# A transformer layer on one core: attention's loop over batches written out, and the next batch's front moved to the first third of a batch

## The reference

```
a  = layernorm(x);  h = rmsnorm(a, norm_w)
q, k, v = h@Wq, h@Wk, h@Wv                         # 16 heads of 8
lin = linear_attention_causal(taylor(q@Wqf), taylor(k@Wkf), v)
win = softmax attention over the last 64 keys
x  = x + a + concat(lin, win) @ Wout               # first half
h2 = layernorm(x)
logits = h2 @ gate_W;  the two best of 8 experts per token, weights by softmax
experts 0..3: gelu MLPs (128-512-128); experts 4..7: two spline layers ("KAN")
x  = x + h2 + weighted sum of the two experts
```

## Time and profile before

| | us |
|---|---|
| median of 3 runs | 1186.65 (1180.09 to 1188.92) |
| span of the profiled execution | 1192.4 |
| PE busy in the span | 887.9 (74%) |
| ACT busy | 552.5 (46%) |
| DVE busy | 521.9 (44%) |
| POOL busy | 509.1 (43%) |

### The profile page before, as it was taken

The page is one execution under the profiler, slowest core; times in us unless marked ns, Lnnn a source line. Parts: engine busy times, 40 slices in busy tenths (PEclk is TensorE's granted clock), DMA queues, the critical chain, the costliest instruction groups (busy, mean ns, idle before and its releaser), DMA issues.

```text
span 1192.4 us, 24590 instructions
## 1 busy us (share of the span) xinstructions
PE 887.9 (74%) x8106; PEld 675.3 (57%) x8107; DVE 521.9 (44%) x2114; ACT 552.5 (46%) x744; POOL 509.1 (43%) x647
## 2 busy tenths in 40 slices
PE   2087897968889698898950277777699988996871
PEld 1055675646656466665630145446487877886770
DVE  5161735527364262736322011112466666575440
ACT  1275563636556364665610142332566565474440
POOL 6050433425333252534133648774445554462222
PEclk9599898979989798998975588898798988998886
DMA  2504032130503204040101245556133241242113
GB/s 55 81 2 73 6 84 23 61 46 2 95 11 78 29 28 78 2 96 9 29 27 25 47 76 76 89 78 163 49 90 90 62 123 46 56 118 64 38 11 86
DMA packets 96202, 68.64 MB, mean 58 GB/s; under 512 B 42892, under 2 KB 87114, under 8 KB 94730
## 3 DMA queue, kind: packets, MB, share of 16 engines
q1 hardware_dynamic: 79210, 55.36, 20.7%
q0 software_dynamic: 16832, 11.09, 6.8%
HBM read 46.86 MB, written 21.37 MB: 57 GB/s over the span
## 4 chain that ended last, share of the span: by engine, by line
PE 32%; POOL 18%; issue 17%; DMA 13%; DVE 6%; ACT 6%; SPq 5%; POOLq 1%; another core or an unknown queue 1%; DVEq 0%; ACTq 0%
POOL acc_d L751 8%; DMA stack<-zeros 6%; PE pv L1449 5%; PE pv L1636 5%; DMA acc_d<-stack,srec 4%; PE ring L1609 4%; PE ring L1371 2%; PE ring L1391 2%; ACT Pb L851 2%; PE ring L1460 2%; PE ring L1412 2%; ACT stack L928 2%; DVE masked L1050 2%; PE ring L1416 2%; POOL stack L741 1%
## 5 line engine op out<-in xcount | busy, mean ns | idle before, releaser
L751 POOL DMA_INDIRECT acc_d<-stack,srec x84 | 136.3, 1623 | 136.8 <-DVE stack L1237 98.1
L1050 DVE CUSTOM_DVE_ANT_0 masked<-ring,mask_max 128x192 bf16<-128x192 f32 (+1 forms) x512 | 141.6, 337 | 114.4 <-PE ring L1371 102.4
L1248 DVE SCALAR_TENSOR_TENSOR stack<-stack 128x512 f32<-128x512 f32 x240 | 158.0, 690 | 43.8 <-ACT stack L928 29.1
L692 POOL TENSOR_SCALAR_AFFINE_SELECT Pb<-Pb 128x1024 f32<-128x1024 f32 x64 | 69.0, 1094 | 218.9 <-ACT Pb L851 160.0
L928 ACT ACTIVATE stack<-ring,kprm 128x512 f32<-128x512 f32 x160 | 111.2, 794 | 107.7 <-DVE stack L1248 105.5
L1449 PE MATMUL pv<-Pb,vaug 128*16 128x128 f32 (+3 forms) x2816 | 142.7, 329 | 22.8 <-issue 22.6
L1636 PE MATMUL pv<-stack 128*128 128x128 f32 x1120 | 136.0, 285 | 17.0 <-DVE stack L1248 9.7
L1636 PEld LDWEIGHTS pv<-stack 128*128 128x128 f32 x1120 | 132.9, 200 | 20.9 <-DVE stack L1248 10.6
L1609 PE MATMUL ring<-stack 128*128 128x256 f32 x560 | 136.9, 409 | 6.0 <-issue 3.8
L1609 PEld LDWEIGHTS ring<-stack 128*128 128x128 f32 x560 | 115.3, 208 | 30.2 <-issue 7.7
L857 ACT ACTIVATE Pb<-ring 128x768 f32<-128x768 f32 x128 | 101.2, 812 | 56.9 <-PE ring L1400 55.6
(11 more groups left out here) (204 smaller groups left out, 1279.7 us busy)
## 6 DMA issues: line engine op xcount, KB each, us to landing
stack<-L_ffn_kan_sl_W SPq DMA_DIRECT2D x20, 1024.0 KB
stack<-hl_d SPq DMA_DIRECT2D x72, 128.0 KB
Pb<-L_ffn_mlp_W SPq DMA_DIRECT2D x22, 256.0 KB
hl_d<-hi SPq DMA_DIRECT2D x7, 384.0 KB, 2.3
hl_d<-lo SPq DMA_DIRECT2D x7, 384.0 KB, 2.9
xb<-L_attn_x SPq DMA_DIRECT2D x9, 256.0 KB
acc_d<-res SPq DMA_DIRECT2D x8, 256.0 KB, 2.5
h_d<-h SPq DMA_DIRECT2D x8, 256.0 KB, 3.1
```

The source lines that it names most:

```text
L751: pool.indirect_dma_start(acc_d, bass.IndirectOffsetOnAxis(ap=srec[:, kind, u, q, 0:1], axis=0), src[:, u % 2, q, :], None, compute_op=ALU ...
L1050: red = dve.tensor_tensor_reduce(masked[:, (NT * n + c) % SLOTS, hh, k0:WQ], slot(job)[:, hh // 2, WQ * (hh % 2) + k0:WQ * (hh % 2 + 1)], ...
L1248: dve.scalar_tensor_tensor(basis[z][:, g % G, :], s_, -1.0, s_, ALU.add, ALU.mult).then_inc(k_bas[z], 1)
```

## The change

- The loop is gone: the eight batches are written out, with constants in place of registers.
- The front's steps stand elsewhere in the list: `stats`, `aggr` and `coef` in the first steps of a batch, `hT` ahead of `out`, then `q`, `k`, `u`, `v`, and `stacks` in the first third, ahead of `h2norm`, `store` and `mT`. `residual` and `xload` stay where they were.
- The DMA of the row of maxima is started by ACT instead of SP, between ACT's copy and the release of the slot.
- POOL does not wait for its records. DVE waits for them itself, in `weights` of the next batch, ahead of overwriting them. POOL's `residual` waits also for its own n of the batch before.
- The padding records are stored by POOL (one DMA of 256 KB) instead of SP, and ACT and DVE wait for that DMA in the prologue beside the other paddings.

```diff
-M L M L M -ytr L M L M L -ycT M L M M -out L L L M -coef2 L M L +stats M +aggr P +coef L L M L L M L
-M M L -h2norm P L +hT -h2T M L -logit L +q L +k mT Y L L -store P L -choose W W W +u +v -rank P
--total W +stacks +residual W -gapexp W W P W Y W W -weights +xload P W W W W Y W W P -scatter P
++stats M L +aggr M L +coef M -ytr L M L M L -ycT M L M M +hT -out L L L M +q -coef2 L M L +k M P L +u L M +v L L
++stacks M L M M L -h2norm P L -h2T M L -logit L L mT Y L L -store P L -choose W W W -rank P
+-total W +residual W -gapexp W W P W Y W W -weights +xload P W W W W Y W W P -scatter P
...
-FIRST = batch_steps(0, False, True)
-TURN = batch_steps(1, True, True) + batch_steps(2, True, True)
-LAST = batch_steps(1, True, False) + [(step, n, 0, 1) for step, n in TAIL]
-TURNS = B // 2 - 1
+PROGRAM = [step for b in range(B) for step in batch_steps(b, b > 0, b < B - 1)]
+PROGRAM += [(step, n, 0, B - 1) for step, n in TAIL]
...
-            sp.dma_start(slot_d.rearrange("(p s) w -> p (s w)", p=P), pad_rec).then_inc(pads_stored, 16)
...
-                    if s == "mT":
-                        sp.wait_ge(mT_ready, batch_no(i, u, 1, 1))
-                        sp.dma_start(stack[p][0][SHIFT_ROW:SHIFT_ROW + 1, :].rearrange("a (h t) -> a h t", h=H),
-                                     mT16[:]).then_inc(mrow_loaded, 16)
...
+            pool.wait_ge(pads_ready, 2)
+            pool.dma_start(slot_d.rearrange("(p s) w -> p (s w)", p=P), pad_rec).then_inc(slots_stored, SLOTS_LEAD)
...
+                        if b > 0:
+                            pool.wait_ge(n2_ready, batch_no(b, 1, 0))
...
-                        pool.wait_ge(slots_stored, batch_no(i, u, 128, 128))
-                        pool.sem_inc(slots_done, 1)
...
+            act.wait_ge(slots_stored, SLOTS_LEAD)
...
+                        act.wait_ge(mT_ready, batch_no(b, 1, 1))
+                        act.dma_start(stack[p][0][SHIFT_ROW:SHIFT_ROW + 1, :].rearrange("a (h t) -> a h t", h=H), mT16[:]).then_inc(mrow_loaded, 16)
                         act.sem_inc(freed[job % SLOTS], 1)
...
-                        dve.wait_ge(slots_done, batch_no(i, u, 1, LEAD))
...
+                        dve.wait_ge(slots_stored, batch_no(b, 128, SLOTS_LEAD))
                         w = rec[:].bitcast(F32)
```

More of the change, by code:

```diff
@@ L323, in slot, with fill_no, wait_filled, wait_freed @@
             return ring[:, job % SLOTS]
[L325 to L354, removed]
+        def fill_no(job):
+            return job // SLOTS + 1
+        def wait_filled(eng, job):
+            eng.wait_ge(filled[job % SLOTS], fill_no(job))
+        def wait_freed(eng, job):
+            if job >= SLOTS:
+                eng.wait_ge(freed[job % SLOTS], job // SLOTS)
+        def batch_no(b, per, off):
+            return b * per + off
         def load_counts(eng):
@@ L497, in batches @@
-                        sp.dma_start(n2_rows[rows].rearrange("a p t d -> (a p) t d"), n2[:]
+                        sp.wait_ge(n2_ready, batch_no(b, 1, 1))
+                        sp.dma_start(n2_rows[b], n2[:]
                                      ).then_inc(rows_stored, 16)
-            all_batches(sp, batches)
+            batches()
             sp.wait_ge(rows_stored, LEAD_DMA + 32 * B)
@@ L590, in _, with link @@
             count = [0]
-            def link(ins, i=0, per=0):
+            def link(ins):
                 count[0] += 1
                 ins.then_inc(pool_chain, 1)
-                pool.wait_ge(pool_chain, i * per + count[0])
-            pool.sem_inc(slots_done, LEAD)
+                pool.wait_ge(pool_chain, count[0])
             pool.memset(ones16[:], 1.0)
@@ L626, in coefficients, with front_coefficients @@
                 pool.tensor_tensor(c[:, 8, :], c[:, 0, :], one, ALU.add)
[L627 to L631, removed]
+                link(pool.tensor_tensor(c[:, 6, :], c[:, 5, :], v, ALU.add))
+                link(pool.tensor_tensor(c[:, 2, :], c[:, 6, :], half, ALU.pow))
+                link(pool.tensor_tensor(c[:, 3, :], c[:, 7, :], c[:, 2, :], ALU.mult))
+            def front_coefficients(bf):
                 pool.wait_ge(stats_ready, bf + 1)
-                coefficients(mv, c1, rms_eps, i, per)
+                coefficients(mv, c1, rms_eps)
             def normed():
@@ L719, in batches @@
                                     rec[:, t, c, :], None).then_inc(slots_stored, 16)
-                        pool.wait_ge(slots_stored, batch_no(i, u, 128, 128))
-                        pool.sem_inc(slots_done, 1)
-            all_batches(pool, batches, count, POOL_PER)
+            batches()
             n_kind = load_counts(pool)
@@ L815, in front @@
                 if s in SPLIT:
-                    if s == "q" and not (isinstance(bf, int) and bf == 0):
+                    if s == "q" and bf > 0:
                         act.wait_ge(hl_stored, bf * 32)
@@ L824, in _ @@
             for s in FRONT:
-                front(s, 0, 0, FRONT.index(s), 0)
+                front(s, 0, 0, FRONT.index(s))
             act.wait_ge(zeroed, 1)
@@ L946, in _, with link @@
             count = [0]
-            def link(ins, i=0, per=0):
+            def link(ins):
                 count[0] += 1
                 ins.then_inc(dve_chain, 1)
-                dve.wait_ge(dve_chain, i * per + count[0])
+                dve.wait_ge(dve_chain, count[0])
             def norm_stats(bf):
@@ L1034, in chain, with batches @@
                 if wait:
[L1035 to L1040 removed]
+                    dve.wait_ge(route_chain, batch_no(b, ROUTE, step[0]))
+            def batches():
+                for s, n, j, b in PROGRAM:
+                    p = b % 2
                     if s in SPLIT:
[L1042 removed]
+                        front(s, b + 1, 1 - p, JOBS[(s, n, 0, b)])
                     if s == "max":
                         c = j
[L1045 to L1046 removed]
+                        job = JOBS[(s, n, c, b)]
+                        wait_filled(dve, job)
                         k0 = WIN if c == 0 else 0
@@ L1324, in _, with front @@
             pe.wait_ge(act_prep, 2)
-            def front(s, bf, u, job, i, jobs):
+            def front(s, bf, job, hT_job):
                 if s == "hT":
@@ L1346, in _ @@
             for s in FRONT:
-                front(s, 0, 0, FRONT.index(s), 0, None)
+                front(s, 0, FRONT.index(s), FRONT.index("hT"))
             for u in range(2):
@@ L1515, in batches @@
                         mm.then_inc(filled[job % SLOTS], 1)
-            all_batches(pe, batches)
+            batches()
             n_kind = load_counts(pe)
```

310 lines of the change are left out of this document (143 added, 167 removed).

## The result

The changed kernel takes 1244.62 us, the median of 4 runs (1241.52 to 1252.76), against 1185.97 for the kernel before on the same chip: ratio 1.0496, 95% interval 1.0438 to 1.0553. It is 5% slower; the forecast was 1168, 1.5% faster. The profiled execution took 1241.52 us, span 1239.7.

What follows compares the result with a forecast made beforehand. PE was taken to bound attention, with idle gaps between batches to take: −28.1 + 2.2 + 7.0 + 1.4 − 1.5 = −19.0 us, profiled 1192.4 to 1173.4, median 1168 us, range 1154 to 1178.

Steps and rivals of the forecast that it cites:

- The starts: Between batches: PE's idle gaps, from the stack's load landing and the loop's turn, all go, 28.1 us gained.
- The row of maxima: Before the first W: the row's DMA on ACT's queue beside a stack load costs 0.2 us a batch, 1.4 in all.
- rival 2: First W of seven batches: the row arrives late behind the load, PE waits 4.8 us each, about 1200 us; chance 0.09.
- The front's products: First third of a batch: q, k, u and v moved there cost 1 us a batch, 7.0 in all, ends -7 and +21.
- hT in batch 0: Batch 0: PE reaches hT's new place before POOL's `hn` is ready and waits, a cost of 2.2 us.
- Prologue: Before the first batch: one padding DMA moves from SP's to POOL's queue, a gain of 1.5 us, bounds 0 and 3.9.
- POOL's and DVE's waits: Records: POOL no longer waits for them and DVE waits in `weights`, most of a batch later; each counted as 0.
- What stays: Last P of batches 1 to 7: still 8 to 9 us instead of 2.6, because of the records; no gain counted.
- rival 3: Batch ends: x1's store behind the stack's load delays records, slow PE reaches the next batch, 7 times 1.8 us, 1180; chance 0.07.
- After attention: The experts' part, behind attention: untouched by the change, no gain counted.

Runs made afterwards that it cites:

- e2: Changed kernel with the earlier order of steps and the row's DMA back on SP, so mainly the loop written out: 1139.35 us, ratio 0.9781 to the kernel before.
- e1: Changed kernel, but SP begins the stack's load only after the batch's row of maxima has landed: 1146.98 us, ratio 0.9923 to the kernel before.
- e3: Changed kernel with the stack's load back in its old place behind the stores: 1151.8 us, ratio 0.9931 to the kernel before.
- e4: Changed kernel loading only three of the stack's nine pieces, results meaningless, only attention read: row landed in 2.1 us, first W never waited.
- g8: g7 with hi and lo stored early and residual and x's load also ahead of the stack's load: 1114.18 us, ratio 0.9691 to the kernel before.
- g9: Changed kernel without the eight indirect DMAs storing a batch's records and DVE's waits for them: first thirds of batches 1 to 6 took 41.8 to 42.5 us.
- h6: The kernel before, unchanged, run again for its trace on a later chip: 1151.19 us.
- g7: e1 with x1's store moved on SP to out's place, ahead of the stack's load: 1126.54 us, ratio 0.9827 to the kernel before.
- h8: The kernel of g8 once more, on another chip: 1120.87 us, ratio 0.9742 to the kernel before.
- h10: g8 with v back in its old place behind the third W: 1110.46 us, ratio 0.9666 to the kernel before.
- g5: The changed kernel again, on a chip where no last P is stretched: 1175.9 us against 1150.42, ratio 1.0249 to the kernel before.

## Why the prediction was wrong

**The starts** (-28.1): right in size. Of the two causes the loop's turn, taken out alone, would have given nothing here: the load takes its place (e2). Their price on another chip would have been twice that, which the earlier trace rows couldn't show: I read the last P's stretch and the gap behind it as two things that add, and they share one limit, the landing of the stacks.

**The row of maxima** (+1.4, the step that failed): the term was mis-sized by a factor of thirty, 44.2 us. The mechanism was named, as rival 2, at 0.09; it came at more than the 4.8 a batch given there, 6.3. The error was to price a DMA beside the load by the earlier trace rows: 5.9 us for eight small DMAs, therefore 0.7 for one. Nothing in the earlier trace rows said that the delay is shared out among the eight. The one row landed 7.6 us later than in the earlier trace rows (9.9 against 2.3), held by the pieces issued before it (e1, e3, e4 and the table of packets). The Trainium skill ("DMA: Bandwidth & Descriptors", Rules for kernel authors) has DMAs of different queues interleave. I took that for a reason why a small one would pass. The trace disagrees with that reading: half of the row moved only about when the last packet of another queue's load did, 4.8 to 9.1 us after the other half.

**The wait's second price** was in no term. Before the change the first W's take 0.33 us, with TensorE's clock at the upper of its two levels (2.4 GHz). After 7.46 us of idle TensorE batch 0's take 0.50 to 0.53, at the lower level (1.2 GHz), until 107; from 109 they take 0.33 again. Windows of batch 0 from the first W to the end of the last P, changed kernel first, then before (the third number from the right is the granted clock):

```profile
103.25:124.76 21.51, 21.51 (x296) 15.46 (x296) 3.62 (x12) 12.56 (x18) 0.00 (x0) 0.91 0.05 8
...
90.58:112.10 21.52, 21.51 (x306) 15.77 (x306) 4.26 (x11) 14.34 (x21) 0.00 (x0) 1.00 0.43 80
```

The stretch of the W is as long as before (153.7) although u's and v's matmuls, 2.2 us a batch, have left it. With no wait it is 148.9 and 149.1 on other chips (e1, g8). Not all of a wait is lost, though: after the waits of 3 us in e3's batches 4 and 5 the stretch is 17.6 instead of 18.8.

**The front's products** (+1 a batch, bounds -1 and +3): 3.5 to 3.9 a batch, above the upper bound. The slot waits alone are 2.4 (I had said that q and u would bring them, and let the pauses swallow them). The other half of the step was wrong too: v's 1.05 was to leave "the stretch where PE is full". There PE's busy time equals the window, but taking u and v out of it shortens it by 0.55 (19.33 in e2, 18.78 in e1, on one chip). In batch 0, which has no tail of another batch, it is 1.8. So another limit lies close behind PE in that stretch, and a busy share of one is not proof that work taken out is time gained.

**hT in batch 0** (+2.2): 1.9. **Prologue** (-1.5): -1.2. **POOL's and DVE's waits** (0): nothing in the traces speaks against it.

**What stays** (the last P's stretch): right, 8.9 to 9.2 us in batches 1 to 6, and right that it belongs to the records. But I stopped at the last P. Their DMAs' semaphores go on rising for 10 us after the last packet (those issued in batch 2 until 288.5, 7.4 us into batch 3). With the gap gone the next batch's first releases fall into this tail and come late: 17 us in batches 2, 3 and 6 on the first chip (46.0, 49.1 and 48.8 against g9's 42.2, 42.0 and 42.5), which no term and no rival had. The tail alone isn't enough. Before the change it reached as far (until 197.7, 7.8 us into batch 2), yet only batch 6, the one start without a gap, had late releases in it, and h6 with its gaps has none; how a gap keeps them away is open. It is the closest to rival 3, whose words were that the slow stretch reaches into the next batch. That rival's cause was the late store of x1. In the changed kernel POOL does wait for it, 63.6 us in all (32.0 before), but its records still wait for DVE after that; only in e1 did the store hold up the next batch, in g7 it was x's load.

**After attention**: the kernel before takes 586.9 and 563.1 us there in its two traces, the changed one 575.6 on the first chip. All kernels with the loop written out and their records stored take 548 to 557 on the later chips (h8 and h10, on the chip of h6's 563.1, 555.8 and 548.4). Some 7 to 15 us are gained on one chip, which I had counted as 0; e2's ratio agrees. Its cause stays open: two traces of the kernel before are too few to place it, and no run took that part by itself.

## What to carry to other kernels

When a large transfer is moved earlier, list everything small that will be issued while it runs, on any queue, and ask of each who waits for it; such a transfer can be held until the pieces issued before it have moved, and its price is not a share of what a group of others paid. Here the same load, begun a few microseconds after the row, x1 and x instead of before them, turned 2.5% slower into 3.1% faster on one chip. Before counting an idle gap as a gain, look at what is still landing at its end.

## What the runs showed of the hardware

TensorE's releases can come 1 to 7 us after the instruction is through while a batch's eight indirect DMAs (128 records each) are under way or landing: some 30 of over 0.6 us in the attention of the changed kernel, some 15 in g5, 12 in g8, none in g9, which has no such DMAs. On the first chip they stretched the last P of batches 1 to 7 by 5.6 to 7.1 us, in the kernel before too. In e2, g5, g8 and h6 on three other chips every last P took 2.51 us, and the late releases fell in the next batch's start or nowhere. What makes the difference between the chips wasn't tried.

A load of nine pieces held exactly half of the packets of another queue's 16 KB DMA, in six of seven batches of the changed kernel until within about 1 us of its own last packet, and a lead of 0.17 us sufficed to cost the first W 3 us (e3).
